# Second attention of a two-layer gated block: the rows of maxima copied in two halves, and the score blocks issued one step sooner

## What is computed

```python
q = _split_heads(Q @ W_Q + b_Q)          # 2 x 16 x 256 x 8
k = _split_heads(K @ W_K + b_K)          # 2 x 16 x 512 x 8
v = _split_heads(V @ W_V + b_V)
scores = jnp.einsum('bhqd,bhkd->bhqk', q, k) * inv_sqrt_dk
weights = jax.nn.softmax(scores, axis=-1)
out = jnp.einsum('bhqk,bhkd->bhqd', weights, v)
```

## Time and profile before

| | us |
|---|---|
| median of 3 runs (lowest to highest) | 169.73 (169.66 to 170.33) |
| profiled execution, its own time | 169.39 |
| its span, first to last instruction | 167.5 |
| TensorE busy in the span | 153.8 (92%) |
| VectorE busy | 105.2 (63%) |
| ScalarE busy | 87.0 (52%) |

### The profile page before, as it was taken

The page is one execution under the profiler, slowest core; times in us unless marked ns, Lnnn a source line. Parts: engine busy times, 40 slices in busy tenths (PEclk is TensorE's granted clock), DMA queues, the critical chain, the costliest instruction groups (busy, mean ns, idle before and its releaser), DMA issues.

```text
span 167.5 us, 3212 instructions
## 1 busy us (share of the span) xinstructions
PE 153.8 (92%) x1188; PEld 98.4 (59%) x1193; DVE 105.2 (63%) x288; ACT 87.0 (52%) x146; POOL 44.6 (27%) x81
## 2 busy tenths in 40 slices
PE   7988988698999889988999999998999979999994
PEld 2446974663548847644444443534536655699993
DVE  1768278797586577999998988981524488102041
ACT  3035636870183045569788787788840276301110
POOL 6442625893760040870000000000200365000000
PEclk9999999689999999999999999999999999999999
DMA  5999999005687987135200000000007000000002
GB/s 147 336 299 407 430 302 184 12 16 138 148 172 145 207 248 274 29 77 72 37 0 0 4 0 0 0 4 0 4 0 250 6 0 0 0 4 0 0 19 57
DMA packets 5858, 16.87 MB, mean 101 GB/s; under 512 B 848, under 2 KB 3536, under 8 KB 5056
## 3 DMA queue, kind: packets, MB, share of 16 engines
q1 hardware_dynamic: 4816, 13.79, 29.9%
q10 hardware_dynamic: 720, 2.44, 4.7%
q0 software_dynamic: 304, 0.40, 0.8%
HBM read 13.94 MB, written 1.25 MB: 91 GB/s over the span
## 4 chain that ended last, share of the span: by engine, by line
PE 73%; DVE 16%; ACT 5%; issue 3%; POOL 1%; ACTq 0%; POOLq 0%; DVEq 0%
PE bank L500 66%; PE bank L504 6%; DVE mx L1468 6%; DVE top L1345 2%; DVE k L1347 2%; ACT arena L1214 1%; POOL rstd L399 1%; PE bank L957 1%; DVE normed L1261 1%; ACT arena L1178 1%; ACT arena L1108 1%; DVE stats L1256 1%; PE bank L680 1%; DVE res_b L1434 0%; ACT attT L1080 0%
## 5 line engine op out<-in xcount | busy, mean ns | idle before, releaser
L1468 DVE TENSOR_REDUCE mx<-bank 128x1 f32<-128x512 f32 x64 | 41.8, 688 | 5.3 <-PE bank L500 4.2
L1178 ACT ACTIVATE arena<-bank 128x1024 f32<-128x1024 f32 x32 | 32.0, 1026 | 8.0 <-PE bank L500 7.5
L500 PE MATMUL bank<-kpack,fc1T_sb 72*128 72x512 bf16 x64 | 22.5, 383 | 0.8 <-DVE mx L1468 0.5
L395 POOL TENSOR_SCALAR rstd<-meanvar 128x2 f32<-128x2 f32 x10 | 2.3, 225 | 71.2 <-DVE meanvar L1257 71.2
L500 PE MATMUL bank<-fc1T_sb,kpack 104*128 104x256 bf16 x128 | 19.3, 272 | 0.1
L500 PE MATMUL bank<-arena,va_flat 128*9 128x256 f32 x256 | 18.0, 381 | 0.2 <-ACT arena L1178 0.2
L500 PEld LDWEIGHTS bank<-fc1T_sb,kpack 104*128 104x128 bf16 x128 | 12.0, 97 | 6.4 <-issue 1.7
L500 PEld LDWEIGHTS bank<-kpack,fc1T_sb 72*128 72x128 bf16 x64 | 6.1, 97 | 11.2 <-issue 5.4
L500 PE MATMUL bank<-selq_bf,quiet 128*128 128x512 bf16 (+2 forms) x46 | 10.6, 348 | 0.4 <-issue 0.2
L500 PEld LDWEIGHTS bank<-arena,va_flat 128*9 128x9 f32 x256 | 5.0, 89 | 7.0 <-issue 4.5
L500 PE MATMUL bank<-kpack,arena 128*128 128x128 f32 (+1 forms) x72 | 8.6, 278 | 0.0
(11 more groups left out here) (231 smaller groups left out, 282.0 us busy)
## 6 DMA issues: line engine op xcount, KB each, us to landing
kpack<-k_parts SPq DMA_DIRECT2D x3, 768.0 KB
fc1T_sb<-in_fc1T SPq DMA_DIRECT2D x1, 2048.0 KB, 13.3
fc_sb<-in_fc SPq DMA_DIRECT2D x1, 2048.0 KB, 17.6
fc_sb<-in_gateup ACTq DMA_DIRECT2D x2, 1024.0 KB, 12.4
kpack<-quiet SPq DMA_DIRECT2D x1, 1024.0 KB, 24.1
arena<-in_down SPq DMA_DIRECT2D x1, 1024.0 KB, 4.8
k_parts<-arena SPq DMA_DIRECT2D x8, 96.0 KB, 2.2
fc1T_sb<-q_rows SPq DMA_DIRECT2D x9, 64.0 KB
```

The source lines that it names most:

```text
L395: pool.tensor_scalar(rstd[:, k, i:i + 2].unsqueeze(2), meanvar[:, k, i:i + 2, 1:2], EPS, None, ALU.add)\
L500: return pe.matmul(o, lhsT, rhs, start=start, stop=stop, **k)
L1178: act.activation(probs1[:, n % (2 * GH), :, :], bank[:, 2 + 2 * (n % 2):4 + 2 * (n % 2), :], ACT.Exp, scale=SCALE)\
L1468: dve.tensor_reduce(mx1[:, b * 2 + qt, g * GH + j:g * GH + j + 1], bank[:, r, :], AX_X, ALU.max)\
```

## The change

The rows of maxima of a unit are copied in two instructions, for two heads each, and each counts up `mrow_sb`. Scores blocks wait for the half that holds their head (every second head waits), and the ring waits for both halves. `SCORE_LAG` goes from 7 to 6, so that every scores block on TensorE, and every exponential on ScalarE, is issued one step sooner. `VALUE_LAG` stays.

```diff
                 elif RING[before[-1]][0] == "max":
-                    pe.wait_ge(S["mrow_sb"], RING[before[-1]][1] + 1)
+                    pe.wait_ge(S["mrow_sb"], 2 * RING[before[-1]][1] + 2)
...
-                if j == 0:
-                    pe.wait_ge(S["mrow_sb"], u + 1)
+                if j % 2 == 0:
+                    pe.wait_ge(S["mrow_sb"], 2 * u + j // 2 + 1)
...
-                        act.copy(qpack[MROW:KROWS, b, g * GH:(g + 1) * GH, :],
-                                 bank[MROW:KROWS, r, 0:SQ].unsqueeze(1).to_broadcast([2 * GH, GH, SQ]))\
-                            .then_inc(S["mrow_sb"], 1)
+                        for h in (g * GH, g * GH + 2):
+                            act.copy(qpack[MROW:KROWS, b, h:h + 2, :],
+                                     bank[MROW:KROWS, r, 0:SQ].unsqueeze(1).to_broadcast([2 * GH, 2, SQ]))\
+                                .then_inc(S["mrow_sb"], 1)
...
-SCORE_LAG = 2 * GH - 1
+SCORE_LAG = 2 * GH - 2
```

## The result

The changed kernel is slower. Its first four executions took 173.31 to 177.38 us, median 175.06, beside 170.03 for the kernel before on the same chip: ratio 1.027, interval 1.022 to 1.032. Two later sets of six on other chips gave medians of 172.87 and 174.24, ratios 1.016 (1.013 to 1.020) and 1.016 (1.009 to 1.022). These comparisons leave out executions marked as disturbed; in the first set that is only the one of 177.38, so its 1.027 still holds one with a lower clock (175.54). I had said 171.9, and 170.4 to 172.6.

What follows compares the result with a forecast made beforehand. It took VectorE's reductions to bound the start, TensorE the body, and partly a ScalarE chain the tail. Terms 1.08 + 0.71 + 1.04 − 0.53 = +2.3 gave a median of 172.0, stated as 171.9 us for likely overlap; range 170.4 to 172.6.

Steps and rivals of the forecast that it cites:

- The split copy: ScalarE's copy of maxima: a half takes 0.58 us, no overlap, first half 0.43 sooner, second 0.18 later.
- The start: Step (1, 2): head 0's block waits for the pack copy and delays the second raw block and its reduction; +1.08 us.
- The same applies in (2, 2), but there VectorE's pace covers it: Step (2, 2): the scores block also waits for the first half copy, but this adds nothing to the time.
- Unit step 3: Step (3, 2): the scores block waits for the first half copy, queued behind an exponential; +0.71 us.
- Unit steps 4 to 7: Waits for the half copies, the ring and the exponential behind the weighted values; +1.04 us, including 0.08 in (4, 0).
- The tail: After the last reduction: two new waits, but the last unit's weighted values start sooner; −0.53 us.
- Eight more ScalarE instructions cost only what is counted.: Whole kernel: the instructions added by splitting the copies cost nothing beyond the terms already priced.
- The clock: Rival, chance 0.03: new stands of 0.7 to 1.1 us halve TensorE's clock for one unit, some 3.4 us; 175.
- Only the start costs: Rival, chance 0.15: the waits of the body hide, leaving +1.08 − 0.53 = +0.55 us; 170.3.
- the short ones don't: Rival, chance 0.15: start and step 3 count, waits of 0.08 to 0.26 us vanish; +1.3, 171.0.
- The sooner blocks fill idle time: Rival, chance 0.04: the earlier blocks use TensorE's 1.0 us of idle time between 72.00 and 78.53; 168.7.

Runs made afterwards that it cites:

- start_undone: The changed kernel with head 0's scores block moved behind both raw blocks of step (1, 2); ratio 1.013 (1.007 to 1.019) to the kernel before.
- value10: The changed kernel with `VALUE_LAG` 10 and nothing else; ratio 1.017 (1.010 to 1.024) to the kernel before.
- late_tail: The kernel before, with the copy ahead of the exponential from unit step 4 and sooner blocks only from (8, 0); 168.89 us, ratio 0.992.
- lag_only: The kernel before with only `SCORE_LAG` shortened to 6, the copy of maxima left whole; ratio 1.029 (1.023 to 1.036).
- padded8: The kernel before with eight unread one-element ScalarE copies added at about 30 us; ratio 1.001 (0.997 to 1.004).

## Why the prediction failed

The direction was right, and so were the mechanisms at the start, in unit step 3 and in the tail. Two steps failed: that the clock holds (chance 0.03 for a fall), and that nothing is lost in (2, 2) and behind the attention. The range was 0.5 us too low even for executions that kept the clock (median 173.1, I had 172.6 as the upper end).

- **The split copy.** 0.575 for a half, as said. I took no overlap; the pair takes 1.06, so the second starts 0.09 before the first ends, and the second half is 0.05 late, not 0.18. The overlap of 93 ns that the Trainium skill (ScalarE: Activation LUTs, section What ACT_TABLE_LOAD costs) gives is what this trace shows; the estimate of 613 ns for a half from its figures is too long by 0.04.
- **The start.** Said +1.08, measured +1.00. The rows came as described; the copies overlap, so all of them are 0.1 sooner. The repair start_undone showed that moving the block by one place takes away half of it (0.54), and that only 0.37 of that reaches w7.
- **"The same applies in (2, 2), but there VectorE's pace covers it."** This step failed. The half copy stands there behind the exponential of (2, 1), which itself comes later with the start, and TensorE stands 0.46; +0.39 not in my sum.
- **Unit step 3.** Said 0.71 for the half copy and 0.08 for (4, 0); measured 0.80 and 0.18, +0.97. The mechanism is right, a size was off: I allowed 0.05 us from the end of one engine's instruction to the start of the other's. That holds for the pack copy (it ends at 75.47, the block goes at 75.53) and for the ring. But a scores block has two waits. Its weight load carries the one for the exponential, and the one for `mrow_sb` is an instruction of its own in TensorE's queue. The half copy begun at 86.60 ends at 87.17, this instruction is through at 87.26 (the packed trace has it at 87.21 for 0.05), the weight load starts at 87.29 and the block at 87.32: 0.14. The exponential's wait for the weighted values is an instruction of its own too: they end at 88.68, it starts at 88.81, 0.13 where I had 0.04.
- **Unit steps 4 to 7.** Said 0.26 a unit, measured 0.27, but by the wrong parts: the sum of 0.18 for the copy with the ring and 0.08 for the exponential is 0.08 and 0.19 by value10. As the copy's second half is hardly late and the block itself goes later, the ring no longer waits at all.
- **The tail.** Said −0.53, measured −0.49.
- **"Eight more ScalarE instructions cost only what is counted."** They cost 0.24 more, behind the attention.
- **The clock.** This step failed too: two of the first four executions fell. As a rival with 0.03 the fall had about the right price (3.4 said, 3.1 measured), but a chance that was some eight times too small: 4 of the 16 executions of the changed kernel fell. It also had the wrong stands. I had thought of the new ones of 0.7 to 1.1; but filling the 0.76 in (1, 2) left three of six fallen, and the one in (3, 2) comes after the fall. What lies between are stands of 0.16, 0.31, 0.33 and 0.30, none longer than those that the kernel before has without a fall. The Trainium skill (TensorE: Matmul & The Clock Gate, section Why this matters for your kernels) speaks of idle gaps between bursts of matmuls. No gap ahead of the fall is longer than 0.8 us here, and none of eighteen executions fell with two of the later ones filled. What exactly the chip looks at stays open.
- **The rivals.** "Only the start costs" is refuted by unit step 3 (+0.97), and both it and "the short ones don't" by the units of 6.95. "The sooner blocks fill idle time" is true of the tail alone, as late_tail shows.

By my own numbers, the two costs left out (0.39 and 0.24) and the undersized waits of step 3 (0.18) are 0.8 us, against a sum that was otherwise 0.1 us too high. That the terms of steps 4 to 7 came out nearly right, with parts that were 0.1 too high and 0.1 too low, was luck.

## What to carry to other kernels

A shorter lag between two stages buys something only where the engine that would wait has idle time; everywhere else each producer that now stands in the same step becomes a wait, so take the shorter lag in the tail alone. Before splitting an instruction to have its first half sooner, look at what it is queued behind: with lag 7 the split cost 0.27 us up to w7, while moving the whole copy ahead of one exponential gained 0.66; with lag 6 the split won 2.5 and the move 1.4 more. Price the wait of a standing engine from rows: here 0.05 us from end to start where the wait sits in the waiting instruction, 0.14 where it is an instruction of its own. And look at all new stands, not only the longest, when asking whether the clock holds.

## What the runs showed of the hardware

- TensorE's clock fell from 2.4 to 1.2 GHz for about 6.9 us (0.57 granted from 80 to 88 us) in both traced executions with a whole clock of 0.971 (changed, lag_only). Ahead of it TensorE was busy for 5.68 of 7.4 us and never stood for more than 0.8 at a time. The granted clocks tell of such a fall in 13 of 38 executions of such kernels; an execution of the changed kernel with the same 5.68 did not fall. None of 18 fell with idle matmuls in two stands.
- A scores block starts 0.06 us after the end of the ScalarE copy that its weight load waits for (75.47 to 75.53), and 0.14 after the end of one that a separate wait instruction guards (87.17 to 87.32).
- Eight ScalarE instructions added at 30 us delay one copy 100 us later by 0.3 us (padded8, 9.34 after w7 instead of 9.04).
- Two ScalarE copies of 8x512 in a row overlap by 0.09 us, but no row shows an overlap between such a copy and the pack copy behind it (73.81 + 1.06 = 74.87, and it starts at 74.89).
